# Fewer matmul increments, and em moved behind e and srq, in a local-attention and spiking feed-forward layer on eight cores

## The reference

```python
def _L0_attn_ref(x, Wg, bg, Wv, bv, Wo, bo):        # WINDOW = 128
    g = x @ Wg.T + bg                                # split into 16 heads
    v = x @ Wv.T + bv
    # per head: corr = cosine of g_i and g_j inside the window, 0 outside
    corr = (corr + 1.0) / 2.0
    denom = jnp.mean(corr, axis=3) + 0.5
    gene_fitness = 1.0 / (denom * jnp.sum(1.0 / denom, axis=2, keepdims=True))
    attn = softmax(corr * gene_fitness[..., None], masked to the window)
    return (attn @ v) @ Wo.T + bo

def _L0_ffn_ref(x, W_fc, W_proj):
    y = jnp.square(jax.nn.relu(x @ W_fc.T)) @ W_proj.T
    # five steps: mem = 0.9*mem + y - (mem > 1); spikes counted, divided by 5

x = x + _L0_attn_ref(_layernorm(x), ...)
x = x + _L0_ffn_ref(_layernorm(x), ...)
```

## Time and profile before

| what | us |
|---|---|
| median of 2 runs | 1674.83 (1669.59 and 1680.08) |
| the profiled execution | 1665.92 |
| its span on the core of the page (core 6) | 1664.2 |
| spans of the 8 cores | 1643.4 to 1664.9 |
| busy: PE, DVE, ACT, POOL | 1030.0, 699.6, 666.2, 130.8 |

### The profile page before, as it was taken

One profiled execution on the slowest core, in us unless ns is written; L12 is line 12 of the kernel. 1 busy time (PEld: TensorE's weight loads), 2 busy tenths in 40 slices (PEclk: granted clock), 3 DMA queues, 4 the chain that ended last, 5 costly groups with the idle time before them and its releaser, 6 DMA issues.

```text
span 1664.2 us, 16422 instructions; the slowest of 8 cores (1643.4 to 1664.9 us)
## 1 busy us (share of the span) xinstructions
PE 1030.0 (62%) x4632; PEld 434.1 (26%) x4632; DVE 699.6 (42%) x1639; ACT 666.2 (40%) x1467; POOL 130.8 (8%) x216
## 2 busy tenths in 40 slices
PE   0024555596466666666657887887788868878800
PEld 0012222242122222222222333332333323333300
DVE  1300222200566666665643020099207940494098
ACT  1354232322366666666664551153305530342000
POOL 1011221111000000000000100110011101111100
PEclk9999787787555555555557998999899989999955
DMA  9978565444100000000004444443544444455301
GB/s 185 227 166 150 93 104 106 101 113 103 25 1 1 1 1 1 1 1 1 1 1 140 125 135 131 129 142 109 192 126 127 152 165 128 125 151 168 110 30 45
DMA packets 78907, 158.68 MB, mean 95 GB/s; under 512 B 38627, under 2 KB 38884, under 8 KB 78820
## 3 DMA queue, kind: packets, MB, share of 16 engines
q0 software_dynamic: 63824, 106.97, 27.0%
q1 hardware_dynamic: 14996, 50.68, 9.2%
HBM read 147.15 MB, written 33.55 MB: 109 GB/s over the span
## 4 chain that ended last, share of the span: by engine, by line
DMA 31%; PE 29%; DVE 14%; ACT 11%; issue 9%; another core or an unknown queue 4%; POOL 1%; DVEq 0%; ACTq 0%; POOLq 0%; SPq 0%
PE psY L834 9%; DMA wpb<-wprojC 7%; PE psY L796 7%; DMA wstg<-wfcT 6%; DMA wfcb<-wfcC 6%; DMA wstg<-wprojT 5%; ACT ebf L526 5%; ACT PT L585 4%; PE psPV L599 4%; DMA wfcC<-wstg 3%; PE psPT L577 3%; DMA wprojC<-wstg 3%; DVE memb L873 2%; DVE t1b L870 2%
## 5 line engine op out<-in xcount | busy, mean ns | idle before, releaser
L796 PE MATMUL psY<-x2nT,wfcb 128*128 128x512 bf16 x1024 | 238.2, 391 | 49.1 <-DMA wfcb<-wfcC 48.0
L834 PE MATMUL psY<-wpb,h_sb 128*128 128x512 bf16 x1024 | 236.2, 387 | 36.9 <-DMA wpb<-wprojC 35.6
L599 PE MATMUL psPV<-PT,v_sb 128*64 128x128 bf16 x512 | 104.2, 307 | 142.0 <-ACT PT L585 142.0
L526 ACT ACTIVATE ebf<-C,fit 128x256 f32<-128x256 f32 x256 | 151.5, 592 | 2.3 <-DVE em L565 0.6
L796 PEld LDWEIGHTS psY<-x2nT,wfcb 128*128 128x128 bf16 x1024 | 99.6, 100 | 186.9 <-issue 82.9
L834 PEld LDWEIGHTS psY<-wpb,h_sb 128*128 128x128 bf16 x1024 | 98.4, 99 | 173.3 <-issue 68.9
L862 DVE TENSOR_SCALAR spkA<-y 128x1024 f32<-128x1024 f32 x16 | 11.2, 697 | 273.7 <-ACT y L852 272.4
L805 ACT ACTIVATE frb<-psY 128x512 f32<-128x512 f32 x128 | 76.7, 599 | 115.3 <-PE psY L796 115.2
L852 ACT ACTIVATE y<-psY 128x512 f32<-128x512 f32 x32 | 16.1, 625 | 263.2 <-PE psY L834 263.2
L565 DVE SCALAR_TENSOR_TENSOR em<-ebf,rqb,maskA_sb 128x256 bf16<-128x256 f32 x240 | 114.7, 481 | 0.9
L478 PE MATMUL psD<-g_sb 64*128 64x256 bf16 x256 | 99.3, 390 | 25.1 <-DMA wprojC<-wstg 21.3
(11 more groups left out here) (99 smaller groups left out, 1193.4 us busy)
## 6 DMA issues: line engine op xcount, KB each, us to landing
wfcb<-wfcC POOLq DMA_DIRECT2D x64, 512.0 KB, 4.2
wpb<-wprojC POOLq DMA_DIRECT2D x64, 512.0 KB, 4.0
xa<-xin SPq DMA_DIRECT2D x32, 512.0 KB, 5.2
wstg<-wfcT POOLq DMA_DIRECT2D x32, 256.0 KB, 5.3
xpair<-xin SPq DMA_DIRECT2D x8, 1024.0 KB, 12.1
wfcC<-wstg POOLq DMA_DIRECT2D x16, 512.0 KB, 3.2
wstg<-wprojT POOLq DMA_DIRECT2D x16, 512.0 KB, 5.5
wprojC<-wstg POOLq DMA_DIRECT2D x16, 512.0 KB, 2.9
```

What stands on the lines that cost most here:

```text
L526: e = b.op("S", lambda h, hb=hb, qt=qt, q4=q4: h.activation(ebf[q4][:], C_sb[hb][:, 256 * qt:256 * qt + 256], AF.Exp, scale=fitb[hb][:, qt ...
L599: mpv = b.op("T", lambda h, h_i=h_i, hp=hp, qt=qt, q4=q4, pb=pb, half=half: h.matmul(psPV[pb][hp:hp + 64, 128 * (q4 % 2):128 * (q4 % 2) + ...
L796: mmt = b.op("T", lambda h, f=f, fp=fp, k=k, gi=gi: h.matmul(psY[f % 2][:], wfcb[fp % 2][:, 1024 * (f % 2) + 128 * k:1024 * (f % 2) + 128 ...
L834: last = b.op("T", lambda h, f=f, f2=f2, tti=tti, nh=nh, pj=pj: h.matmul(psY[pj][:], h_sb[:, 512 * f + 128 * tti:512 * f + 128 * tti + 128 ...
```

## The change

Two things. First, the matmuls that are not the last of their group no longer increment PE's semaphore: `inc=0` but for the last of four transposes, the last of eight matmuls over the chunks, the second half in `emit_pt` and `emit_pv`, and in the second feed-forward product the last of the eight matmuls on a hidden chunk (for the last chunk all eight). The waits stay as they are. Second, in the attention loop em of step i-19 is emitted behind e and srq of step i-17 in place of ahead of them.

```diff
@@ -289,7 +289,8 @@
...
                     x1n[i][:, 128 * c:128 * c + 128], ident_sb[:],
                     start=True, stop=True),
-                    waits=[tok_x1n, psT_free[j], tok_pre])
+                    waits=[tok_x1n, psT_free[j], tok_pre],
+                    inc=1 if c % 4 == 3 else 0)
@@ -318,7 +319,8 @@
...
                     wgT_sb[:, 1024 * k + 512 * nh:1024 * k + 512 * nh + 512],
                     start=(k == 0), stop=False),
-                    waits=[tok_wg, x1T_toks[tt], psG_free[gi]])
+                    waits=[tok_wg, x1T_toks[tt], psG_free[gi]],
+                    inc=1 if k == NC - 1 else 0)
@@ -361,7 +363,8 @@
...
                     ghat[i2][:, 128 * c:128 * c + 128], ident_sb[:],
                     start=True, stop=True),
-                    waits=[tg, psT_free[j]])
+                    waits=[tg, psT_free[j]],
+                    inc=1 if c % 4 == 3 else 0)
@@ -384,7 +387,8 @@
...
                     wvT_sb[:, 1024 * k + 512 * nh:1024 * k + 512 * nh + 512],
                     start=(k == 0), stop=(k == NC - 1)),
-                    waits=[tok_wv, x1T_toks[tt], psV_free[vi]])
+                    waits=[tok_wv, x1T_toks[tt], psV_free[vi]],
+                    inc=1 if k == NC - 1 else 0)
@@ -578,7 +582,7 @@
...
                 em_sb[q4][:, 128 * half:128 * half + 128], ident_sb[:],
                 start=True, stop=True),
-                waits=[em_tok[q4], psPT_free[q4]])
+                waits=[em_tok[q4], psPT_free[q4]], inc=half)
@@ -602,7 +606,7 @@
...
                 start=(half == 0), stop=(half == 1),
                 tile_position=(0, hp)),
-                waits=[pt_ev[pb], tok_v, psPV_free[q4]])
+                waits=[pt_ev[pb], tok_v, psPV_free[q4]], inc=half)
@@ -623,12 +627,12 @@
             emit_pass1(*hq(i))
         if i >= 22 and i - 22 < NSTEP:
             emit_pv(*hq(i - 22))
-        if i >= 19 and i - 19 < NSTEP:
-            emit_em(*hq(i - 19))
         if i >= 17 and i - 17 < NSTEP:
             emit_e(*hq(i - 17))
             if (i - 17) % NT % 2 == 1:
                 emit_srq(hq(i - 17)[0], hq(i - 17)[1] - 1)
+        if i >= 19 and i - 19 < NSTEP:
+            emit_em(*hq(i - 19))
@@ -714,7 +718,8 @@
...
                     woT_sb[:, 1024 * c + 512 * nh:1024 * c + 512 * nh + 512],
                     start=(c == 0), stop=False),
-                    waits=[tok_pv, tok_wo, psY_free[pw]])
+                    waits=[tok_pv, tok_wo, psY_free[pw]],
+                    inc=1 if c == NC - 1 else 0)
@@ -771,7 +776,8 @@
...
                         x2n[li][:, 128 * c:128 * c + 128], ident_sb[:],
                         start=True, stop=True),
-                        waits=[x2n_tok[li], psY_free[pj]])
+                        waits=[x2n_tok[li], psY_free[pj]],
+                        inc=1 if c % 4 == 3 else 0)
@@ -798,7 +804,8 @@
...
                     x2nT[:, 2048 * k + 512 * gi:2048 * k + 512 * gi + 512],
                     start=(k == 0), stop=(k == NC - 1)),
-                    waits=[tok_wf[fp % 2], x2nT_toks[-1], psY_free[f % 2]])
+                    waits=[tok_wf[fp % 2], x2nT_toks[-1], psY_free[f % 2]],
+                    inc=1 if k == NC - 1 else 0)
@@ -836,7 +843,8 @@
...
                         start=(f == 0), stop=(f == NF - 1)),
                         waits=[tok_wp[f2 % 2], h_toks[f],
-                               psY_free[pj] if f == 0 else None])
+                               psY_free[pj] if f == 0 else None],
+                        inc=1 if (f == NF - 1 or (tti == 3 and nh == 1)) else 0)
```

## The result

| | before | after |
|---|---|---|
| median, us (runs) | 1670.4 (42) | 1681.1 (43) |
| ratio after to before, 95% interval | | 1.0057 (1.0039 to 1.0075) |
| span on the core of the page, us | 1664.2 | 1669.5 |
| attention, first PT copy to last x1T copy, median of 8 cores, us | 432.6 | 444.8 |
| ahead of it, us | 432.9 | 430.4 |

The change makes the kernel slower by 0.57%, 9.5 us on 1670 (6.5 to 12.5). The medians are over all runs; the ratio leaves out those in which the cores of a die ran longer at a lower granted clock. Attention, read from the trace of each core as the time from the start of the first copy of PT to the start of the last copy x1T, grows by 12.2 us; over the 8 cores it lies between 432.4 and 433.3 before and between 444.6 and 445.0 after. The other two stretches move by 2 us in opposite directions.

What follows compares the result with a forecast made beforehand. Attention was taken to be paced by a loop between PE and ACT, 3.17 us a turn. Increments at zero plus 11.2 us over 15 head ends, on the 1674.8 median, gave 1686 us, range 1670 to 1699.

Steps and rivals of the forecast that it cites:

- Part 1: Dropping 3254 semaphore increments across the kernel: claimed worth zero, at most the whole 0.09 us of a handoff.
- A normal pair: Pair of tiles inside a head: em and its transpose come 0.27 us later, hidden by 0.36 us before PT; costs nothing.
- 0.21 us at the end of a head: After a head's last C and em, denomb starts later on DVE and delays psS through to the next e: 0.21 us.
- The pair behind it: First pair after a head's end: late s_sb delays em, transpose and PT; 0.88 us even, 0.59 odd, the 0.21 included.
- The wait of s_sb: DVE's idle time before s_sb, waiting for e in a pair: to grow from 0.72 to about 1.1 us.
- some 15 waits of PE for em by over 0.5 us: Attention: PE was to wait for em some 15 times, each by over 0.5 us.
- 670.65 for 670.38: Trace time in us at which a normal pair's second transpose starts on PE, forecast after the change against before.
- A sign of being wrong that was set too tight: On DVE in attention: the prediction is wrong if em starts sooner than 0.1 us behind rqb.
- The other two signs: Prediction wrong if turns inside a head lengthen, or if the feed-forward stretch gets shorter by more than 5 us.
- every pair pays: Rival: the transpose's 0.27 us reaches PT in each of 113 pairs, 30.5 us more, 1717 us; chance 0.08.
- nothing comes through: Rival: the delay at the end of a head is hidden too, 1675 us; chance 0.14.
- the increments hold nothing: Denies the rival that increments held handoffs in attention and weight-slice waits: 16 us gained, 1670 us; chance 0.06.

Runs made afterwards that it cites:

- the kernel with PV later: PV taken two steps later (i-24) and em behind e and srq, against the same with em ahead: attention 408.0 us in place of 354.1.

## Why the prediction was right, point by point

- **Part 1 at zero.** Right. Attention is the same to 0.1 us with and without the 3254 increments, in either order, and in the feed-forward product the distance from the first matmul of a run to ACT and to POOL is the same with eight increments and with one. The page of the Trainium skill, "TensorE: Matmul & The Clock Gate", section "The cost: per-tile semaphore tail", would by the prediction's estimate from its figure have given about 28 us. What it states of tiles that run concurrently was not tested here; no run here shows a cost for matmuls that follow each other.
- **A normal pair at zero, with 0.36 us of cover.** Right: inside a head the turns stay, and the two kernels with more work ahead of em put the edge of the cover where it was worked out, within about 0.05 us.
- **0.21 us at the end of a head.** Right on average: 0.20 us, that is 0.24 in even heads and 0.15 in odd ones, where 0.21 was taken for both.
- **The pair behind it.** Even heads 0.88 forecast, 0.87 in the pair shown (5.14 us against about 5.15) and 0.85 in the mean. Odd heads 0.59 forecast and 0.59 in the mean, but that is in part luck. Of the seven odd ends after, four take 4.87, which is 0.53 above the 4.34 usual before. Two take 5.2 us and one 4.69. In one of the two longer ones rsib, in the other em starts 0.3 us or more later than elsewhere, on all 8 cores alike; why, and why one is shorter, stays open. Ends altogether 11.2 us forecast, 10.9 measured.
- **What was left out.** The end of attention: in the last head a turn near the end goes from 2.40 to 2.87 us, and the turn that follows the last stats by 0.3 us from 2.85 to 3.19. These steps issue no psD and C and the turns are shorter; that the cover is smaller there was not tested. With small changes in the turns behind each end they make up the 1.3 us between 10.9 and 12.2.
- **The wait of s_sb.** Forecast to grow from 0.72 to about 1.1 us; it is 0.91. Moving em behind s_sb takes 0.40 us of work from ahead of the wait, but the C and em of the step before also come 0.21 us later. The prediction used that 0.21 for the end of the head and forgot it here. It also forecast some 15 waits of PE for em by over 0.5 us. There are 39: the 15 at the ends (1.2 us and more), one of 0.55 to 0.9 us in each turn behind an end, which it had not seen, and nine in and around the last head and at the start. The other 89 are nearly all of 0.24 us and cost nothing inside a head; they follow from its own 670.65 for 670.38, and weren't spoken of.
- **A sign of being wrong that was set too tight.** em was not to start sooner than 0.1 us behind rqb, and it starts 0.09 us behind it. The sign was the 0.10 of the earlier trace rows without room for a hundredth; nothing hangs on it. The other two signs didn't come: turns inside a head stay, and what lies behind attention takes 790.5 us against 788.9.
- **The time.** 1686 us was 1674.8 + 11.2. The median after is 1681.1 with the one before now at 1670.4 on more runs: the step is 10.7 us by the medians, 9.5 by the ratio. So the base was 4.4 us too high, which is noise of two runs, and the step was right. Attention alone grew by 12.2, 1.0 more than the sum: the terms left out add 1.3, and the ends came 0.3 below it.

Of the rivals, "every pair pays" is false by the turns inside a head, though in the kernel with PV later, where the cover is gone, the pairs inside heads pay 42 of the 54 us; "nothing comes through" is false by the ends; and the increments hold nothing.

## What to carry to other kernels

An operation that doesn't need the result of a wait belongs ahead of it in an engine's list: behind the wait it costs nothing as long as something slower covers it, and the cover ends where the pattern is broken, here at the end of each head. Look for the loop that sets the pace (who waits for whom, in both directions), cut it by taking one of its operations a few steps later, and expect orders that were free before to cost after that: 12 us became 54. Increments that nobody waits for are free here; taking them out is no optimization.

## What the runs showed of the hardware that was not expected

Forecast, but shown here for the first time by experiment: an increment on every 128x512 matmul leaves the step at 0.216 us and the distance from the first of eight to ACT's start at 1.98 us, the same as with one increment for eight.

In heads whose PV result goes to partitions 64 to 127, a turn takes 3.45 us in place of 3.16. Most of the time lies on ACT: from the start of x1T to that of e 0.50 us in place of 0.37, from e to PT 0.72 in place of 0.59. In the timeline of the changed kernel, an even head (its PT at 670.67 is shown above) and an odd one:

```profile
669.71 0.47 ACT L612 ACTIVATE x1T<-psPV,bvp_sb 64x256 bf16<-64x256 f32 x1 [1.05 <-PE psPV L603]
...
670.08 0.59 ACT L530 ACTIVATE ebf<-C,fit 128x256 f32<-128x256 f32 x1
...
697.86 0.47 ACT L612 ACTIVATE x1T<-psPV,bvp_sb 64x256 bf16<-64x256 f32 x1 [1.06 <-PE psPV L603]
...
698.36 0.60 ACT L530 ACTIVATE ebf<-C,fit 128x256 f32<-128x256 f32 x1
...
699.07 0.60 ACT L589 ACTIVATE PT<-psPT 128x512 bf16<-128x512 f32 x1
```

With PT directly behind x1T the difference of the turns is 0.14 us in place of 0.29. In the odd heads g is read from the upper 64 partitions as well. Which of the operations is slowed by the position, and by what, was not tested.
